# Two node stages of a graph network: transposes and copies one node block ahead, rows two chunks behind, counts applied after the product

## The reference, cut to what matters

```
x = layernorm(x + gnn0(x, ...))
x = layernorm(x + gnn1(x, ...))
# gnn0 ends: agg = segment_sum(alpha * h, dst);  out = node + agg @ blockdiag(Wps, Wpv)
# gnn1 begins: f = x @ blockdiag(Wl1), sc = x @ blockdiag(Wsc), both times node_attr
# gnn1 ends: mean = segment_sum(mid, dst) / clip(count, 1)
#            out = sc + (mean @ Wa) * (mean @ Wl2) * node_attr^2 / (64 + 32)
```

## Time and profile before

| | us |
|---|---|
| median of 3 runs (lowest to highest) | 8936.91 (8934.33 to 8939.71) |
| the profiled execution's own time | 8938.71 |
| its span in the trace | 8936.9 |
| PE busy in the span | 7365.5 (82%) |
| DVE busy | 7148.1 (80%) |
| ACT busy | 5177.2 (58%) |
| POOL busy | 5377.7 (60%) |

### The profile page before, as it was taken

One profiled execution on the slowest core, in us unless ns is written; L12 is line 12 of the kernel. 1 busy time (PEld: TensorE's weight loads), 2 busy tenths in 40 slices (PEclk: granted clock), 3 DMA queues, 4 the chain that ended last, 5 costly groups with the idle time before them and its releaser, 6 DMA issues. The chain is left out here.

```text
span 8936.9 us, 205108 instructions
## 1 busy us (share of the span) xinstructions
PE 7365.5 (82%) x44896; PEld 5510.5 (62%) x44897; DVE 7148.1 (80%) x17617; ACT 5177.2 (58%) x15797; POOL 5377.7 (60%) x5220
## 2 busy tenths in 40 slices
PE   0968888888888888888884777797878888888878
PEld 0457777777777777777774666554444444444457
DVE  2459999999999999999997566533777788888865
ACT  3246666666666666666662111132777788888852
POOL 0047777777777777777771655300777777666610
PEclk9989999999999999999996999855999999999975
DMA  5334433333333333333332777722444444444433
GB/s 236 89 74 104 104 104 104 104 104 104 104 104 104 104 104 104 105 104 104 104 104 70 210 201 190 146 73 67 117 120 119 123 125 126 119 118 116 115 109 101
DMA packets 1029295, 1036.44 MB, mean 116 GB/s; under 512 B 434719, under 2 KB 846239, under 8 KB 1028127
## 3 DMA queue, kind: packets, MB, share of 16 engines
q0 software_dynamic: 225792, 385.65, 18.3%
q1 hardware_dynamic: 498672, 373.76, 15.3%
q10 hardware_dynamic: 304784, 276.49, 9.3%
HBM read 685.76 MB, written 349.49 MB: 116 GB/s over the span
## 5 line engine op out<-in xcount | busy, mean ns | idle before, releaser
L1708 POOL DMA_INDIRECT f_e<-table,f_src x1568 | 1603.3, 1023 | 539.1 <-issue 418.5
L681 POOL DMA_INDIRECT e_g_src<-table_src,e_idx x1568 | 1609.1, 1026 | 505.0 <-issue 477.6
L681 POOL DMA_INDIRECT e_g_dst<-table_dst,e_idx x1568 | 1605.9, 1024 | 477.8 <-issue 370.3
L1761 PE MATMUL f_ps_a<-f_q,f_onehot 128*128 128x384 f32 x3936 | 1435.2, 509 | 107.1 <-DVE f_q L1846 104.2
L1761 PEld LDWEIGHTS f_ps_a<-f_q,f_onehot 128*128 128x128 f32 x3936 | 722.0, 193 | 581.8 <-DVE f_q L1846 121.6
L1311 PE MATMUL r_ps<-r_h,r_onehot 128*128 x3936 | 694.0, 320 | 208.3 <-DVE r_onehot L1275 76.3
L805 ACT ACTIVATE e_m1t<-e_ps_t 128x512 f32<-128x512 f32 (+1 forms) x1176 | 657.7, 592 | 293.6 <-PE e_ps_t L718 269.7
L1257 POOL TENSOR_TENSOR r_h<-r_h,logits 128x656 f32<-128x656 f32 x392 | 503.1, 1287 | 534.7 <-DMA r_h<-edge_values 533.9
L1311 PEld LDWEIGHTS r_ps<-r_h,r_onehot 128*128 128x128 f32 x3936 | 578.0, 194 | 324.5 <-issue 324.4
L1794 ACT ACTIVATE f_wy<-f_ps_w,f_y 128x96 f32<-128x96 f32 x1968 | 509.9, 342 | 454.3 <-DVE f_q L1846 113.4
L718 PE MATMUL e_ps_t<-ident,e_m1v 128*128 128x128 f32 x3136 | 515.8, 287 | 249.3 <-ACT e_m1t L805 122.0
(11 more groups left out here) (273 smaller groups left out, 18715.9 us busy)
## 6 DMA issues: line engine op xcount, KB each, us to landing
edge_values<-e_h ACTq DMA_DIRECT2D x392, 330.0 KB
r_h<-edge_values SPq DMA_DIRECT2D x392, 330.0 KB, 3.9
sums<-f_acc ACTq DMA_DIRECT2D x492, 192.0 KB
f_rbf<-basis SPq DMA_DIRECT2D x492, 96.0 KB
sums<-r_acc ACTq DMA_DIRECT2D x492, 82.5 KB, 3.4
basis<-b_part SPq DMA_DIRECT2D x48, 784.0 KB, 6.7
e_rbf<-basis SPq DMA_DIRECT2D x392, 96.0 KB
e_g_src<-table_src,e_idx POOLq DMA_INDIRECT x1568
```

Of the source, the lines that this page charges most:

```text
L681: pool.indirect_dma_start(out=into[:, r, t, :], out_offset=None, in_=table, in_offset=bass.IndirectOffsetOnAxis(ap=idx[:, r, c:c + 1], axi ...
L1708: pool.indirect_dma_start(out=rows_of_units[:, place * T + t, :], out_offset=None, in_=table, in_offset=bass.IndirectOffsetOnAxis(ap=src[: ...
L1761: last = nc.tensor.matmul(ps_a[slot][:, 0:ACC1], onehot[:, r, t, :], q[:, r, t, :], start=t == 0, stop=t == T - 1)
```

## The change

In both stages PE now turns block n+1 before it multiplies block n, over chunk borders too. ACT copies block n+1 once the product of block n-1 is done, and moves block n after that. The slot of a block alternates over chunk borders, so that there is one more parity to keep. The wait of PE for all moves at a chunk's start is gone.

In `middle` the two copies become one, of all 128 partitions and 256 columns (DVE clears the unused part of `pt` once); PE goes averages(c), rows(c-2) instead of averages(c), rows(c-1); DVE's average(c+1) lies inside normalise(c-1), between its variance and its root; the root lies in the rows pass; SP loads sums two chunks and x one chunk ahead. At the end rows(12) and rows(13) follow each other.

In `final` PE turns the sums themselves. The tile `means` and the pass over it are gone; ACT multiplies by share as it moves a product to `conv`. gain * conv + resid is one instruction for each block, seven for each chunk. SP waits for the transposes before it loads sums, and for `ADDED` of chunk c-2 before it loads resid and factor; it waits for the finished chunk c-2 only before the store.

The core of the diff (bookkeeping of counts, slots and the first and last chunks left out):

```
@@ middle, ACT
+            def copy(n, slot):
+                act.wait_ge(turned, n + 1)
+                wait(act, multiplied, n - 1)
+                nc.scalar.activation(turned_rows[:, slot, :], pt[slot][:, 0:2 * P], ACT.Copy).then_inc(copied, 1)
...
+                for b in range(CHUNK):
+                    n, slot = first + b, (b + parity) % 2
+                    if b < CHUNK - 1 or not last:
+                        copy(n + 1, 1 - slot)
+                    if b == root_at:
+                        roots(of)
+                    act.wait_ge(multiplied, n + 1)
+                    move(b, po[slot]).then_inc(moved, 1)
@@ middle, PE
+                for b in range(CHUNK):
+                    n, slot = first + b, (b + parity) % 2
+                    if b < CHUNK - 1:
+                        turn_one(b + 1, 1 - slot)
+                    else:
+                        turn_next(1 - slot)
+                    pe.wait_ge(copied, n + 1)
+                    wait(pe, moved, n - 1)
...
+                if within(c - 2):
+                    averages(c, r, lambda slot: turn_rows(c - 2, r, 0, slot))
+                    rows(c - 2, r, 1, next_average if within(c + 1) else oldest_rows)
@@ middle, SP
+                load_sums(c + 2, r)
+                load_x(c + 1, 1 - r)
                 wait(sp, completed, (c - 1) * COMPLETE)
-                store(c - 2, r)
+                if within(c - 2):
+                    store(c - 2, r)
                 sp.dma_start(factor[:, r], factor_d[c]).then_inc(factor_in[r], 16)
@@ middle
-        ROOT_AT = 4
+        ROOT_AT, FIRST_ROOT_AT, LAST_ROOT_AT = 2, 4, 5
@@ final
-        ROOT_AT = 4
+        ADDED = 1 + CHUNK
+        ROOT_AT = 5
@@ final, SP
-                wait(sp, averaged, (c - 1) * MEANS)
+                wait(sp, turned, (c - 1) * CHUNK)
                 sp.dma_start(sums[:, r], sv[c]).then_inc(sums_in[r], 16)
-                wait(sp, finished, (c - 1) * FINISH)
+                if not isinstance(c, int) or c >= 2:
+                    sp.wait_ge(finished, (c - 2) * FINISH + ADDED)
                 sp.dma_start(resid[:, r], rv[c]).then_inc(rest_in[r], 16)
                 sp.dma_start(factor[:, r], factor_d[c]).then_inc(rest_in[r], 16)
+                wait(sp, finished, (c - 1) * FINISH)
                 store(c - 2, r)
@@ final, ACT
+                    if b == 0:
+                        act.wait_ge(shared, (c + 1) * SHARE)
+                        wait(act, finished, (c - 1) * FINISH)
+                    nc.scalar.activation(conv[:, r, b, :], po[slot][:, 0:1 + D], ACT.Copy,
+                                         scale=share[:, r, b:b + 1]).then_inc(moved, 1)
@@ final, DVE
-                dve.wait_ge(averaged, k2)
-                d.up(nc.vector.tensor_tensor(means[:, r], sums[:, r], bc(share[:], 2, ACC1), ALU.mult))
...
-                dve.wait_ge(finished, d.up(nc.vector.tensor_tensor(z[:], conv[:, r, :, 1:1 + D], bc(gain[:], 2, D),
-                                                                   ALU.mult)))
-                dve.wait_ge(finished, d.up(nc.vector.tensor_tensor(z[:], z[:], resid[:, r, :, 0:D], ALU.add)))
+                for b in range(CHUNK):
+                    k = d.up(nc.vector.scalar_tensor_tensor(z[:, b, :], conv[:, r, b, 1:1 + D], gain[:, b:b + 1],
+                                                            resid[:, r, b, 0:D], ALU.mult, ALU.add))
```

More of the change, by code:

```diff
@@ L1454, in roots, with blocks @@
             def roots(c):
[L1455 to L1473, removed]
+                act.wait_ge(normed, c * NORM + SPREAD)
+                nc.scalar.activation(root[:], stat[:, 0:CHUNK], ACT.Sqrt).then_inc(rooted, 1)
+            def copy(n, slot):
+                act.wait_ge(turned, n + 1)
+                wait(act, multiplied, n - 1)
+                nc.scalar.activation(turned_rows[:, slot, :], pt[slot][:, 0:2 * P], ACT.Copy).then_inc(copied, 1)
+            def blocks(first, parity, move, root_at=None, of=None, last=False):
+                for b in range(CHUNK):
[6 more added lines that the diff above has]
+                    move(b, po[slot]).then_inc(moved, 1)
             def averages(c, r):
@@ L1479, in move, with rows @@
                     return nc.scalar.activation(proj[:, r, b, :], bank[:, 0:D], ACT.Copy)
[L1481 to L1485, removed]
+                first_one = isinstance(c, int) and c == 1
+                blocks(base(c), r if isinstance(c, int) and c < 2 else 0, move,
+                       FIRST_ROOT_AT if first_one else None, 0)
+            def rows(c, r, j, parity, root_at, of, last=False):
                 def move(b, bank):
@@ L1525, in rows @@
[L1525 to L1528, removed]
-            def body(c, r, j):
[L1531 to L1536, removed]
+            pe.wait_ge(cleared, 2)
@@ L1558, in average, with normalise @@
                 assert d.n == AVERAGE
-            def normalise(c, r, j):
-                if not present(c):
+            def normalise(c, r, j, between):
+                if not within(c):
                     return
@@ L1966, in _, with turn, product @@
             pe.wait_ge(weights, 48)
-            def product(n, slot, all_moved):
+            def turn(c, r, j, b, slot):
+                if b == 0:
+                    pe.wait_ge(sums_in[r], (j + 1) * 16)
+                for k in range(4):
+                    last = nc.tensor.transpose(pt[slot][0:MID, k * P:(k + 1) * P],
+                                               sums[:, r, b, k * MID:(k + 1) * MID], ident[:])
+                last.then_inc(turned, 1)
+            def product(n, slot):
                 pe.wait_ge(copied, n + 1)
-                wait(pe, moved, n if all_moved else n - 1)
+                wait(pe, moved, n - 1)
                 rows, into = turned_rows[:, slot, :], po[slot]
@@ L1981, in body @@
             def body(c, r, j):
[L1982 to L1992, removed]
+                for b in range(CHUNK):
+                    slot = (b + r) % 2
+                    if b < CHUNK - 1:
+                        turn(c, r, j, b + 1, 1 - slot)
+                    elif not isinstance(c, int) or c < chunks - 1:
+                        turn(c + 1, 1 - r, j + r, 0, 1 - slot)
+                    product(c * CHUNK + b, slot)
+            turn(0, 0, 0, 0, 0)
+            in_pairs_to_last(pe, chunks, body)
         @block.scalar
```

194 lines of the change are left out of this document (123 added, 71 removed).

## The result

The changed kernel takes 8678.11 us (median of 4 runs, 8650.47 to 8705.77), the kernel before 8936.23: a ratio of 0.9711, 95% interval 0.9673 to 0.9748. 8825 was forecast, 8806 to 8862 the range.

The account below looks back on a forecast made before the run. PE was taken to bound both stages, thinly delayed by ACT's copy and chunk borders. Gains of 56 (`middle`), 55 (`final`) and 0.9 (tail), 112 off 8938.7, gave 8826.8; the median 1.8 lower, 8825 us, range 8806 to 8862.

Parts of the forecast that it names:

- A transpose pair behind a product: Two transposes up to the next product, without a wait for the copy: 0.48 us at least, taken as 0.50.
- low bounds of the text: Least time from transposes to the next product: 0.48 us for a pair in `middle`, 0.85 for four in `final`.
- 1.77, 1.28 and 1.73: Microseconds of the product itself in a rows block, an averages block and a `final` block, carried over unchanged.
- Rival 1: Transpose-to-product distance stays, being the product's own weight load, so only the borders go: 8858 us, 14%.
- 2.27 + 1.78: Forecast microseconds of a rows block plus an averages block in `middle`, 98 of each; `middle` gains 56.
- rival 2: Denser PE work raises the clock from 0.50 to 1.00: 8685 us with `middle`, 8615 with `final` too, 7%.
- x1 of chunk 13: At the end of `middle`, rows(13) waits for x1, whose root comes late: 0.7 us lost.
- The borders: PE's standstill at chunk borders; in `final` 2.27 us for DVE's pass over the sums, expected to go.
- The first load of `final` to its transpose: Start of `final`: the first transpose waits for the first sums alone, taken as 6.5 us, at most 10.4.
- rival 4: A new wait for share or a late root, 1 to 3 us a chunk: 8840 to 8865 us, 8%.
- Rival 3: Copies and products don't run side by side, so each product is held up: slower, 8958 us, 3%.
- The seven instructions: DVE's work for z behind the last block of `final`: 1.8 us instead of 2.72, a gain of 0.9 once.

Follow-up runs that it names:

- mid_copy_late: The changed kernel with ACT copying each block of `middle` only after the product before it: 8842.9 us, ratio 0.9885 to the kernel before.
- fin_copy_late: The changed kernel with each copy in `final` alone held back until the product before it is done: ratio 0.9802 to the kernel before, `final` 261.4 us.
- mid_only: The changed `middle` with the old `final`: 8751.72 us, ratio 0.9777 to the kernel before.
- changed_again: The changed kernel itself, run once more: 8678.27 us, ratio 0.9687 to the kernel before.
- changed_third: The changed kernel itself, run again in a group whose edge stages took longer: 12160.9 us, ratio 0.9764 to the kernel before.
- before_fill_mm: The kernel before with one added float32 product of the identity per block of `middle`, in PE's gap: ratio 0.9899, `middle` 327.3 us.
- averages_copy_late: The changed kernel with copies held back until the product before is done, in the averages passes of `middle` only: ratio 0.9879 to the kernel before.
- before_warm: The kernel before with 48 products of the identity on PE ahead of `middle`: ratio 0.9992.
- warm_both: The changed kernel with 48 products of the identity ahead of `middle` and 20 ahead of `final`: ratio 0.9786 to the kernel before.
- fill_start: The changed kernel with one added product of the identity per block in the first two averages passes of `middle`: 8702.37 us, ratio 0.9703 to the kernel before.

## Why the prediction was wrong, step by step

**The blocks: the product was mis-sized.** "A transpose pair behind a product is then 0.27 + 0.21 = 0.48": measured 0.27 + 0.21 in `middle` and 0.86 in `final`, at or within 0.01 of the low bounds of the text. But 1.77, 1.28 and 1.73 for the product itself were carried over as they stood, and it measured 1.61, 1.13 and 1.56. Their first weight load had been exposed inside them; with the copy early it runs beside a transpose. Rival 1 saw this load and looked for it between transpose and product; part of it was in the product. `mid_copy_late` and `fin_copy_late` show it by putting back the copy alone: 1.29 and 1.72 again. The prediction had "every other engine under two thirds", which leaves PEld out: its loads filled 38.73 of 50 us in `final`. Size, at the lower clock: 2.27 + 1.78 against 3.70 is 0.35, times 98 is 34 us in `middle`; 2.61 against 2.43 is 18 us in `final`.

**The clock: rival 2 happened in `middle`, not in `final`.** It had 7%, and was worth 117.8 us in the profiled execution (by the same estimate 84 to 126 in `mid_only`, `changed_again` and `changed_third`). The step that failed is its counter-argument, "400 us at 47.87 of 50 busy never raised it, and 4 us in 50 is all that is added". It took the busy time of the profile's page for what the clock sees, and `before_fill_mm` stands at 1.00 with 47.42 of 50. The rule of the Trainium skill ("TensorE: Matmul & The Clock Gate", section "Part 1: The HAM clock gate") that sustained activity releases the throttle spoke for the rise, and `middle` agrees with its direction. `final` does not plainly: PE busy 40.00 of 40 at 0.50. The price of rival 2 was near: 140 us at the higher clock throughout was forecast, with a chunk of 18 us; the fast chunks took 7 x (0.93 + 1.16) = 14.6, and the first 66 us were low.

**What held.** ACT and DVE kept up: in `middle` PE waited for DVE once behind the start, 4.3 us for x1 of chunk 13 (0.7 was forecast, for the lower clock, at which DVE has nearly twice the time), and the clock fell within this wait. The borders went. The first load of `final` to its transpose took 6.5 us, as taken. No new wait for share, nor one for a root in every chunk: rival 4 is out. Rival 3 is out too: each product now shares its time with a copy and is shorter. The seven instructions took 2.16 rather than 1.8, against two passes of 2.72: 0.6 us.

**The sum.** 112 forecast; + 34 + 18 for the blocks, + 118 for the clock, + 5.0 for the start, - 7.7 for the edge stage, and about - 0.5 for the tail give 279. Without the clock it would still have been 161, some 8776: below the range by the blocks alone. So both steps failed: the price of the product and the argument against the clock.

**What stays open.** What the clock goes by. Shown is: it rose in `middle` only with early copies in the rows passes, or with added products; added transposes in the old order did not do it; and the same program rose after 47, 66 and 92 us, versions of it after 8 to 199. That this spread makes the scatter of the times (8650 to 8706) agrees with the mean clocks of the four executions above; only one of the four was traced. Why `final` never rises, with PE busy throughout and filled further, was not found, nor whether it would keep a high clock that it started with. Whether the waits made the clock fall was not tested either: in `middle` each fall but those of `averages_copy_late` came in a wait of PE or at its end, two at the stage's very end aside. Moving up the x1 of chunk 13 was not tried.

## What to carry to other kernels

Issue the copy that feeds a product one block ahead: it takes away the wait and, besides, the product's first weight load, 0.12 and 0.16 us of 1.89 here. Look at PEld as well as at PE: where a load starts only with its product, it can move. When a sum rests on products that stood behind a wait, price them without their first load. And where PE runs at 0.50 with small stalls in each block, give a rise of the clock real weight, even if the page already says 9 of 10 busy: in `middle` it was worth 118 us here, the order itself 91.

## What was not expected of the hardware

- Adding work made a kernel faster: one product a block, in a gap, `middle` 453.6 to 327.3. One transpose in the same gap did nothing (453.7).
- PE "busy" 40.00 of 40 us can hold 0.28 us of stall in each 1.89 us block.
- At one and the same busy share (47 to 48 of 50) `middle` stood at 0.50 in one kernel and at 1.00 in another.
- Where PE came to a wait of 2.8 to 4.3 us at the higher clock, the clock was at 0.50 within 1 us of the wait's end or earlier (`agg` in `before_warm`, `warm_both` and `fill_start`, the sums in `warm_both`, x1 of chunk 13), so the warm-ups ahead of a wait were lost here.
